# Newton's steps on GpSimd, the attention's sum first, and the context's tiles in other places of a round

## The reference

```python
Pn = rmsnorm(P, input_norm_w)                  # P: the context, 8 x 1601 x 512
k_proj = Pn @ Wk.T;  v_proj = Pn @ Wv.T
for _ in range(3):
    sn = rmsnorm(slots, slot_norm_w)           # slots: 8 x 64 x 512
    q_proj = sn @ Wq.T
    scores = jnp.einsum('bkd,bmd->bkm', q_proj, k_proj) * SCALE
    attn = jax.nn.softmax(scores, axis=-2)     # over the 64 slots
    attn = attn / (jnp.sum(attn, axis=-1, keepdims=True) + EPS)
    updates = jnp.einsum('bkm,bmd->bkd', attn, v_proj)
    slots = gru_cell(updates, slots, gru_wih, gru_whh, gru_bih, gru_bhh)
```

## Time and profile before

| | us |
|---|---|
| median of 3 runs | 1064.41 |
| lowest, highest | 1062.46, 1066.25 |
| the profiled execution | 1069.95 |
| its span | 1068.2 |
| TensorE busy in it | 888.7 (83%) |
| VectorE, ScalarE, GpSimd busy | 653.2, 359.8, 10.0 |
| rounds 1 to 12 | 148 to 741 |

### The profile page before, as it was taken

The page is one execution under the profiler, slowest core; times in us unless marked ns, Lnnn a source line. Parts: engine busy times, 40 slices in busy tenths (PEclk is TensorE's granted clock), DMA queues, the critical chain, the costliest instruction groups (busy, mean ns, idle before and its releaser), DMA issues. The chain is left out here.

```text
span 1068.2 us, 38071 instructions
## 1 busy us (share of the span) xinstructions
PE 888.7 (83%) x17686; PEld 720.6 (67%) x17686; DVE 653.2 (61%) x1288; ACT 359.8 (34%) x651; POOL 10.0 (1%) x34
## 2 busy tenths in 40 slices
PE   3586678888899898889879898866798768999998
PEld 1433678888899888889879788765457535444443
DVE  3676357885876867776848776444426745455543
ACT  2564424332524324433315311111245423423320
POOL 2000000000000000000000000000000000000000
PEclk9899789999899899899989999898895886899999
DMA  9748750054280271560370634112041003133201
GB/s 340 266 91 164 233 103 3 4 113 154 41 201 30 47 184 39 91 176 4 65 201 4 100 109 98 27 66 95 5 96 40 10 21 99 60 119 99 89 9 39
DMA packets 157734, 99.70 MB, mean 93 GB/s; under 512 B 128845, under 2 KB 141189, under 8 KB 154381
## 3 DMA queue, kind: packets, MB, share of 16 engines
q1 hardware_dynamic: 150720, 94.68, 34.3%
q10 hardware_dynamic: 6540, 2.63, 0.9%
q0 software_dynamic: 320, 0.03, 0.0%
HBM read 59.84 MB, written 2.88 MB: 59 GB/s over the span
## 5 line engine op out<-in xcount | busy, mean ns | idle before, releaser
L905 PE MATMUL score<-qa,unit 128*128 128x64 f16 (+1 forms) x2496 | 122.5, 197 | 31.7 <-DVE scratch L676 21.4
L890 PE MATMUL score<-qa,ctxT 128*128 128x64 f16 x3744 | 123.9, 198 | 25.2 <-DVE qa L646 18.5
L905 PEld LDWEIGHTS score<-qa,unit 128*128 128x128 f16 (+1 forms) x2496 | 119.2, 101 | 29.9 <-issue 29.9
L890 PEld LDWEIGHTS score<-qa,ctxT 128*128 128x128 f16 x3744 | 120.6, 102 | 27.5 <-DVE qa L646 19.8
L841 PE MATMUL gate<-qa,Bt 128*128 128x64 f16 x3456 | 116.3, 200 | 16.0 <-DVE qa L687 16.0
L841 PEld LDWEIGHTS gate<-qa,Bt 128*128 128x128 f16 x3456 | 113.8, 103 | 16.9 <-DVE qa L687 16.9
L905 PE MATMUL score<-scratch,unit 128*128 128x64 f16 (+1 forms) x1248 | 120.6, 197 | 3.2 <-issue 3.2
L905 PEld LDWEIGHTS score<-scratch,unit 128*128 128x128 f16 (+1 forms) x1248 | 114.4, 101 | 7.1 <-issue 7.1
L841 PEld LDWEIGHTS gate<-hs,whhT 128*128 128x128 f16 x3456 | 108.5, 98 | 13.2 <-issue 7.8
L841 PE MATMUL gate<-hs,whhT 128*128 128x64 f16 x3456 | 110.6, 194 | 6.8 <-issue 6.8
L1632 PE MATMUL e_hid<-e_xs,e_ws 128*128 128x512 f16 x480 | 110.1, 391 | 0.0
(11 more groups left out here) (216 smaller groups left out, 1281.6 us busy)
## 6 DMA issues: line engine op xcount, KB each, us to landing
unit<-in_ctx_dram SPq DMA_DIRECT2D x24, 1024.0 KB, 9.6
ctxT<-in_L_ffn_routed_w_dram SPq DMA_DIRECT2D x24, 512.0 KB, 3.9
ctxT<-in_L_xattn_gru_wih_dram SPq DMA_DIRECT2D x3, 1024.0 KB, 17.6
ctxT<-in_L_xattn_gru_whh_dram SPq DMA_DIRECT2D x1, 3072.0 KB, 25.9
ctxT<-in_L_attn_Wqkv_dram SPq DMA_DIRECT2D x12, 256.0 KB, 8.5
ctxT<-in_L_ffn_shared_w_dram SPq DMA_DIRECT2D x6, 512.0 KB, 6.3
tail<-in_ctx_dram SPq DMA_DIRECT2D x8, 130.0 KB
unit<-in_L_xattn_Wq_dram SPq DMA_DIRECT2D x1, 1024.0 KB, 5.7
```

Source lines behind the costliest of these rows:

```text
L890: mm = pe.matmul(score[n][:, t * K:(t + 1) * K], a, q, start=(k == 0), stop=(k == 3 * DC - 1), skip_group_check=True)
L905: mm = pe.matmul(score[n][:, dc * K:(dc + 1) * K], a, q, start=first, stop=True, skip_group_check=True)
```

## The change

- `rsqrt` of the slots' and the rows' norms leaves VectorE. VectorE makes the argument and the seed (`seed`, `root_seed`), GpSimd the rest in ten dependent instructions (`rsqrt_on`: one step of third order and one of second), and `q_out` and ScalarE's tiles wait for it. The queue of GpSimd is slot_root(1), norms at "w4", slot_root(0), norms at "w7". The layer norms keep the old function.
- TensorE sums the squares of the slots in a part of its own, `slot_squares`: for lane 1 after four tiles of scores(0), for lane 0 where it was, ahead of query(0).
- The attention's sum is update's first product, in columns 960:1024 of the lane's tile (before the last one, in 256:320). VectorE adds epsilon and inverts it in `total_out`, for lane 0 between softmax_shift(1) and softmax_norm(1), for lane 1 after w3 and ahead of update_out(1).
- Tiles and norms get other places. Odd batches, round m = 0: w2 tiles 0 and 1 (was 0 to 3), w3 2 and 3 (was 4 to 7), w7 4 to 7 (was 8 and 9, and now ahead of q_out); round m = 1: w1 8 and 9, w1b 10 to 12 (was w1 10 to 12). Even batches: w1 tile 0 and w1b 1 to 3 (was w1 0 to 3). Between w1 and w1b VectorE has seed(1). Norms of an odd batch go from w2 to w4, of an even one from w1 of round m = 2 to w7 of the round before.

```diff
+def root_seed(dve, st, v, y, ready):
+    dve.tensor_scalar(y.bitcast(I32), v.bitcast(I32), -0.5, MAGIC, ALU.mult, ALU.add).then_inc(ready, 1)
+def rsqrt_on(pool, st, v, y, t, u, ready):
+    st.after(st(pool.tensor_tensor(t, y, y, ALU.mult)))
+    st.after(st(pool.tensor_tensor(t, t, v, ALU.mult)))
+    st.after(st(pool.tensor_scalar(u, t, 0.375, -1.25, ALU.mult, ALU.add)))
+    st.after(st(pool.tensor_tensor(t, t, u, ALU.mult)))
+    st.after(st(pool.tensor_scalar(t, t, 1.875, None, ALU.add)))
+    st.after(st(pool.tensor_tensor(y, y, t, ALU.mult)))
+    st.after(st(pool.tensor_tensor(t, y, y, ALU.mult)))
+    st.after(st(pool.tensor_tensor(t, t, v, ALU.mult)))
+    st.after(st(pool.tensor_scalar(t, t, -0.5, 1.5, ALU.mult, ALU.add)))
+    pool.tensor_tensor(y, y, t, ALU.mult).then_inc(ready, 1)
...
-            spans = ({"w2": (0, 4), "w3": (4, 8), "w7": (8, 10)}, {"w1": (10, MT)},
-                     {"w1": (0, 4), "w4": (4, 6), "w2": (6, 10), "w3": (10, MT)})[m]
+            spans = ({"w2": (0, 2), "w3": (2, 4), "w7": (4, 8)}, {"w1": (8, 10), "w1b": (10, MT)},
+                     {"w1": (0, 1), "w1b": (1, 4), "w4": (4, 6), "w2": (6, 10), "w3": (10, MT)})[m]
...
-            b = {(2, "w1"): 2 * k + 2, (0, "w2"): 2 * k + 1}.get((m, place), B)
+            b = {(1, "w7"): 2 * k + 2, (0, "w4"): 2 * k + 1}.get((m, place), B)
...
+            norms(0)
+            slot_root(0, 1)
+            norms(1)
+            slot_root(1, 1)
+            slot_root(0, 2)
+            for r in range(1, ROUNDS):
+                if r > 1:
+                    slot_root(1, r)
+                for name in ("w4", "w7"):
+                    if name == "w7" and r + 2 < ROUNDS:
+                        slot_root(0, r + 2)
+                    if norms_in(r, name) is not None:
+                        norms(norms_in(r, name))
...
+            def total_out(n, step):
+                r = attn_sum[n]
+                dve.wait_ge(total_done[n], step)
+                st.after(st(dve.tensor_scalar(r, score[n][:, 960:1024], RMS_EPS * AS, None, ALU.add)))
+                return st(dve.reciprocal(r, r))
...
             def one_round(r):            # VectorE
                 both = r + 1 < ROUNDS
                 place(r, "w1")
+                if r > 1:
+                    seed(1, r)
+                place(r, "w1b")
...
                 softmax_shift(1, r)
+                if both:
+                    inverted = total_out(0, r + 1)
                 softmax_norm(1, r)
                 if both:
-                    update_out(0, r + 1)
+                    update_out(0, r + 1, inverted)
+                row_norms(r, "w4")
...
                 place(r, "w3")
-                update_out(1, r)
+                inverted = total_out(1, r)
+                update_out(1, r, inverted)
+                if r + 2 < ROUNDS:
+                    seed(0, r + 2)
+                row_norms(r, "w7")
+                place(r, "w7")
                 if r + 2 < ROUNDS:
                     q_out(0, r + 2)
-                place(r, "w7")
...
             def update(n, step):         # TensorE
+                pe.wait_ge(attn_summed[n], step)
+                pe.matmul(score[n][:, 960:1024], c.ones32[:], attn_sum[n], start=True, stop=True, skip_group_check=True)\
+                    .then_inc(total_done[n], 1)
...
-                pe.wait_ge(attn_summed[n], step)
-                mm = pe.matmul(score[n][:, 256:320], c.ones32[:], attn_sum[n], start=False, stop=True, skip_group_check=True)
...
                     hidden_rz(0)
-                    scores(0, r + 1)
+                    scores(0, r + 1, 0, 4)
+                if r > 1:
+                    slot_squares(1, r)
+                if both:
+                    scores(0, r + 1, 4, MT)
```

More of the change, by code:

```diff
@@ L158, in recurrence @@
         h_next = sb("h_next", [P, DC, K])
-        ssq, rrow, rtmp = (sb(name, [P, MT]) for name in ("ssq", "rrow", "rtmp"))
+        ssq, rrow, rtmp, rpoly = (sb(name, [P, MT]) for name in ("ssq", "rrow", "rtmp", "rpoly"))
         vecs = sb("vecs", [P, 2 * DC])
@@ L174, in recurrence @@
         rowsum = [scratch[:, n, 912:912 + MT] for n in range(2)]
-        root = [scratch[:, n, 832:1024].rearrange("p (j k) -> p j k", j=3) for n in range(2)]
+        root = [scratch[:, n, 768:1024].rearrange("p (j k) -> p j k", j=4) for n in range(2)]
         q32 = [scratch[:, n, 256:512].rearrange("p (c k) -> p c k", c=DC) for n in range(2)]
@@ L407, in _, with norms, slot_root @@
                     pool.tensor_tensor(c.pick[:, part], c.pick[:, part], one_of(other), ALU.add).then_inc(picks, 1)
+            st = Steps(pool, pool_done)
+            def norms(b):
+                pool.wait_ge(rows_seeded, b + 1)
+                rsqrt_on(pool, st, ssq[:], rrow[:], rtmp[:], rpoly[:], normed)
+            def slot_root(n, step):
+                v, y, t, u = (root[n][:, j] for j in range(4))
+                pool.wait_ge(seeded[n], step)
+                rsqrt_on(pool, st, v, y, t, u, rooted[n])
+            norms(0)
[11 more added lines that the diff above has]
+                        norms(norms_in(r, name))
         @block.scalar
@@ L634, in slots_low, with seed, q_out @@
                 dve.tensor_tensor(hs[n][:, 1], src, hs[n][:, 0], ALU.subtract).then_inc(h_lo[n], 1)
-            def q_out(n, step):
-                v, y, t = (root[n][:, j] for j in range(3))
+            def seed(n, step):
+                v, y = (root[n][:, j] for j in range(2))
                 dve.wait_ge(sq_summed[n], step)
                 st.after(st(dve.tensor_scalar(v, score[n][:, 448:512], WS * WS / D, RMS_EPS * WS * WS, ALU.mult, ALU.add)))
-                rsqrt(dve, st, v, y, t)
+                root_seed(dve, st, v, y, seeded[n])
+            def q_out(n, step):
+                y = root[n][:, 1]
+                dve.wait_ge(rooted[n], step)
                 dve.wait_ge(q_done[n], step)
@@ L774, in _ @@
             norms(0)
+            seed(0, 1)
             q_out(0, 1)
@@ L787, in _ @@
             low_tiles(1, 0, 3)
-            update_out(0, 1)
+            update_out(0, 1, total_out(0, 1))
             low_tiles(1, 3, 5)
@@ L793, in _ @@
             slots_low(0, 2)
+            seed(1, 1)
+            seed(0, 2)
             q_out(0, 2)
@@ L843, in chunks, with slot_squares @@
                 return mm
-            def query(n, step):
+            def slot_squares(n, step):
                 pe.wait_ge(h_sq[n], step)
@@ L852, in query @@
                 mm.then_inc(sq_summed[n], 1)
+            def query(n, step):
                 pe.wait_ge(h_hi[n], step)
@@ L877, in hidden_n, with scores @@
                 hidden(n, 8, GC)
-            def scores(n, step):
+            def scores(n, step, first=0, end=MT):
                 b = 2 * ((step - 1) // ITERS) + n
-                pe.wait_ge(q_split[n], step)
-                waited = 0
-                for t in range(MT):
-                    while waited < len(TURNS) and (t == 0 and waited == 0 or lo_at(t) >= TURNS[waited - 1][1]):
-                        pe.wait_ge(tile_turned[n][waited], (b // 2 + 1) * 16)
-                        waited += 1
+                if first == 0:
+                    pe.wait_ge(q_split[n], step)
+                for t in range(first, end):
+                    for g in range(len(TURNS)):
+                        if (t == 0 and g == 0) or (t > 0 and g > 0 and lo_at(t - 1) < TURNS[g - 1][1] <= lo_at(t)):
+                            pe.wait_ge(tile_turned[n][g], (b // 2 + 1) * 16)
                     k = 0
@@ L966, in _ @@
             inputs(0, 1)
+            slot_squares(1, 1)
             query(1, 1)
+            slot_squares(0, 2)
             query(0, 2)
```

21 lines of the change are left out of this document (13 added, 8 removed).

## The result

| | median us | range, runs | ratio to the kernel before |
|---|---|---|---|
| kernel before | 1063.43 | 1061.19 to 1066.25, 4 | |
| changed kernel | 1034.93 | 1032.95 to 1036.77, 4 | 0.973, 95% interval 0.970 to 0.976 |

A forecast was written before the change was run, and what follows sets the result against it. The prediction took TensorE's program to bound a round, leaving its waits and the slow products behind them to win. Terms 17.0 + 15.3 - 15.6 + 2.5 - 4.8 = 14.4 us gave 1050 us from a median of 1064.41, range 1032 to 1072.

The forecast's parts named there:

- A: Rounds 1, 2, 5, 8: TensorE's long waits for the query's low half and slow products behind them go; +17.0 us.
- B: Rounds 3, 6, 9: fewer tiles ahead of candidate(0), so inputs(1) begin 4.7 us earlier; 3 x 5.1 = +15.3 us.
- C: Rounds 4, 7, 10: late context transposes hold TensorE in scores(1), and lane 0's root is longer; 3 x 5.2 = -15.6 us.
- D: Rounds 11 and 12, without tiles: less waiting for the query and behind the update's last product; +2.5 us.
- E: Ahead of round 1: norms and roots one after the other on GpSimd make TensorE wait longer; -4.8 us.
- the clock's: TensorE's waits: slow products follow only the four long ones, 6.6 us in all; waits under 1 us cost nothing more.
- the forecast wait: Rounds 4, 7, 10: TensorE waits 4.3 us at tile 8 in scores(1) for the third transpose, landing at T + 20.0.
- The root's part: End of the round before rounds 4, 7, 10: lane 0's longer root beside four tiles, taken as 0.9 us each.
- (2): Rival, chance 0.13: the context's third transpose is not late, or overlaps the second; gain 34, 1030 us.
- (3): Rival, chance 0.14: half of the 32 us saved returns as TensorE's waits without releaser; 1066 us.
- (4): Rival, chance 0.19: GpSimd's step is too long, at 0.50 us a step roots delay TensorE by 25 us; 1075 us.

The follow-up runs named there:

- late_start: Changed kernel with the squares' product back right ahead of the queries and the seeds ahead of the queries' scaling, roots still on GpSimd; 1068.16 us (1.003).
- root_on_dve: Changed kernel with all roots computed by VectorE's old steps at the place of the new seeds, none on GpSimd; 1037.87 us (0.977).
- small_turns: Changed kernel with each batch's 26 halves turned in six transposes of 4 or 5 halves instead of three; 1019.21 us (0.9595).

## Why the prediction was half right

By terms, from the starts of the rounds in the two profiles (us gained):

| term | forecast | profile |
|---|---|---|
| A: rounds 1, 2, 5, 8 | +17.0 | +21.0 |
| B: rounds 3, 6, 9 | +15.3 | +21.8 |
| C: rounds 4, 7, 10 | -15.6 | -12.5 |
| D: rounds 11, 12 | +2.5 | +2.4 |
| E: ahead of round 1 | -4.8 | -3.5 |
| sum | 14.4 | 29.2 |

**The step that failed is the clock's.** The forecast said "Waits under 1 us cost nothing more" and charged slow products only behind the three-microsecond waits: 6.6 + 1.2 gained in A and B, 4.5 taken off in C, so about 3 us. The rows show 20.8 us less busy time for the same products (by the noise of the clock told above, some us of it may not be the change's). Idle time came out the other way, 12.3 us in the eleven rounds where the other terms had about 16. In round 3 the wait ahead of inputs(1) was 1.53 us (forecast 2.0) and these began at T + 42.2 (forecast 42.5), but then ran at full clock, where I had gained only 0.4 us on them. Behind 1.91 us of waiting such a row had taken 5.92 us before; the changed kernel's row of round 3:

```profile
281.43 4.37 PE L915 MATMUL gate<-qa,Bt 128*128 128x64 f16 x144 [1.53 <-DVE qa L746]
```

I had priced the clock wait by wait. It would have been nearer, if read from the busy time of whole stretches: 45.98 us in a round at 0.90 against 41.59 at 1.00 is 4.4 us per round of m = 0 or 2.

- **A, the path.** Right: the query's wait went but for 1.7 us, all in round 1, root 3.78 for 3.7 (5.0 where tiles run beside it), and late_start brings the wait back.
- **B.** Right in the events of round 3 to within 0.5 us, too small by the clock.
- **C.** The price is real and near the forecast size in sum (6.4, 1.9 and 4.2 us for 5.2 each), its label was wrong for two of the three rounds. The third transpose came as late as worked out; I had not seen that TensorE would be late too, from late instruction blocks and the 0.50 clock behind them. Where fewer of them hold it up, the forecast wait shows: 7.8 us in three rounds of root_on_dve, 0.9 us in round 4 of small_turns. The root's part (5.38 us beside the tiles, against 6.3 if every step waits) was hidden in round 4 behind the 2.14 us of issue wait. Round 4 is still longer than rounds 2 and 3 in small_turns (46.7 us against 44.2 and 45.1); how much of that is the root's, no run separates.
- **D and E.** D is right in sum only (round 11 gained 3.0 us, round 12 lost 0.6). E cost 3.5 us where 4.8 were forecast; root_on_dve measured it by itself, 3.6 us.
- **Rivals.** (2) named 1030 us, near the time, but by "third transpose not late", and this did not happen: C came out at -12.5, not +3.9. (3) was true in half: 11.3 us of waits came back without releaser, of 16. What beat it was the clock. Its words "these waits sit beside the context's transfers" held the largest lever of the kernel, 15 to 18 us by one line, and I used it only as a discount. (4) needed a step of 0.50 us; clean ones take 0.24 to 0.37, and only the nine roots beside tiles come to 5.0 or 5.4 us.
- **Open.** That the waits which went gave back the clock is argued, not shown. Why the clock differs so between kernels isn't settled by their idle time: late_start is idle for 81.5 us of its eleven rounds (561.60 less 480.13 busy) at a clock of 0.95, the kernel before for 68.1 at 0.93.

## What to carry to other kernels

Price TensorE's granted clock from busy time per stretch, for the same number of products, not from single waits: here the same products were busy for up to 20.8 us less, while idle time fell by 12.3. And read it against the clock of a stretch that the change doesn't touch, which moved by 5.5 us of busy time here. Waits without a releaser that end 1.2 to 1.7 us after an instruction packet are a limit of their own, beside large DMA transposes and loads; cut the transposes (here from 8 or 9 halves to 4 or 5) before anything is rearranged around them, and stop where waits for data take over. In moving a short dependent chain to GpSimd, first ask what the same early start would give on VectorE: here all but 3 of the 28.5 us.

## What the runs showed of the hardware

- Transposing DMAs of 8 or 9 halves cost TensorE up to 2.3 us at a time, though it waits for their data in one round only. With them gone, 22.3 us went; with each halved, 15.7.
- Instruction packets of 16 KB usually start 4.0 us apart and take about 1 us. Each wait of TensorE without releaser ended 1.2 to 1.7 us after one had landed; in the changed kernel these had started 5.4 to 10.1 us after the one before.
- A transpose of 8 or 9 halves landed 7.2 to 9.8 us after its issue (changed kernel, all of them), one of 4 or 5 halves 4.3 to 7.4 (small_turns).
- GpSimd's dependent step on 128x64 f32 takes 0.24 us with a constant (0.37 in one place) and 0.29 to 0.32 with two operands, with gaps of 0.09. Beside VectorE's operation on two SBUF operands it takes 0.65 to 0.73, while VectorE's own median is 751 ns against 747.
- A one-operand VectorE operation took 0.50 us (mean) for 512 elements in even rows and slowed GpSimd's steps; 511 elements in 7 rows took 737 ns and didn't.
